# A first stage with a longer table ring, a normalisation split around the gates, and new orders on three engines

## The reference, cut to what matters

```python
x = x + 0.5 * ffn(layernorm(x))          # 8 experts of rank 16, top-2 gates
x = x + attn(layernorm(x))               # 16 heads of 16, relative positions
x = x + 0.5 * ffn(layernorm(x))

def ffn(x):                              # tokens x 256
    topw, sel = top_k(x @ Wg, 2)         # Wg 256x8
    cw = sum(one_hot(sel) * softmax(topw))
    return einsum('ter,erd->td', einsum('td,edr->ter', x, A) * cw[..., None], B)

def attn(w):
    q, k, v = w @ Wq.T, w @ Wk.T, w @ Wv.T   # split into 16 heads
    rp = sin_table(2 * L - 1, 256) @ Wr.T    # the projected table of positions
    s = (q + u_bias) @ k.T + rel_shift((q + v_bias) @ rp.T)
    return softmax(s / 4) @ v
```

## Time and profile before

| | us |
|---|---|
| median of three runs | 3110.54 |
| lowest, highest | 3108.45, 3118.55 |
| profiled execution, device time | 3110.02 |
| its span in the trace | 3108.2 |
| start of phase 1, of phase 2 (TensorE's F1) | 71.50, 98.13 |
| start of phase 8 (TensorE's P1) | 264.21 |
| last store issued by stage one | 287.70 |
| TensorE, VectorE, ScalarE, GpSimd busy, share of the span | 93%, 85%, 80%, 75% |

### The profile page before, as it was taken

One profiled execution on the slowest core, in us unless ns is written; L12 is line 12 of the kernel. 1 busy time (PEld: TensorE's weight loads), 2 busy tenths in 40 slices (PEclk: granted clock), 3 DMA queues, 4 the chain that ended last, 5 costly groups with the idle time before them and its releaser, 6 DMA issues. The chain is left out here.

```text
span 3108.2 us, 110074 instructions
## 1 busy us (share of the span) xinstructions
PE 2887.8 (93%) x40768; PEld 2036.2 (66%) x40768; DVE 2630.9 (85%) x5042; ACT 2500.7 (80%) x3854; POOL 2315.8 (75%) x4135
## 2 busy tenths in 40 slices
PE   6674699999999999999999999999999999999966
PEld 3452377777777777767677777777776767677645
DVE  4763399998999999989898999999998989899977
ACT  3443689888888898978888888889888988898832
POOL 4443888888888888878887888888887888788820
PEclk8886699999999999999999999999999999999987
DMA  6446888888888888878888888888888888888751
GB/s 202 153 130 164 203 218 229 223 231 219 225 226 228 226 228 223 229 206 223 230 221 224 224 230 228 226 221 231 228 227 213 227 229 225 218 229 227 208 155 55
DMA packets 290292, 657.40 MB, mean 212 GB/s; under 512 B 189536, under 2 KB 256992, under 8 KB 272352
## 3 DMA queue, kind: packets, MB, share of 16 engines
q0 software_dynamic: 190960, 526.89, 64.5%
q1 hardware_dynamic: 98800, 123.38, 13.7%
HBM read 77.19 MB, written 46.14 MB: 40 GB/s over the span
## 5 line engine op out<-in xcount | busy, mean ns | idle before, releaser
L834 POOL DMA_DIRECT2D score<-score x3999 | 2183.4, 549 | 499.6 <-ACT score L1093 430.2
L1091 ACT COPY score<-pos_bank 128x512 f32<-128x512 f32 x2048 | 1104.7, 597 | 280.2 <-PE pos_bank L967 278.2
L1101 ACT ACTIVATE score<-score,low 128x1024 f32<-128x1024 f32 x1024 | 1197.0, 1170 | 34.0 <-DVE low L1154 30.7
L1163 DVE COPY prob_t<-pt_bank 128x512 f32<-128x512 f32 x1792 | 1161.1, 683 | 5.1 <-PE pt_bank L1033 4.9
L1033 PEld LDWEIGHTS pt_bank<-ident_sb,score 128*128 128x128 f32 x8192 | 952.4, 142 | 217.1 <-issue 45.3
L1033 PE MATMUL pt_bank<-ident_sb,score 128*128 128x128 f32 x8192 | 1085.3, 275 | 9.0 <-issue 7.0
L1154 DVE CUSTOM_DVE_ANT_0 score<-ac_bank,score 128x1024 f32<-128x1024 f32 x512 | 626.8, 1224 | 253.6 <-PE ac_bank L1019 125.1
L1154 DVE CUSTOM_DVE_ANT_0 score<-ac_bank,score,low 128x1024 f32<-128x1024 f32 x512 | 657.0, 1283 | 57.2 <-PE ac_bank L1019 48.4
L967 PE MATMUL pos_bank<-pos,qv 96*32 96x512 bf16 (+15 forms) x12160 | 659.8, 317 | 28.7 <-DMA qv<-qv_parts 25.6
L1047 PE MATMUL acc_bank<-prob_t,vs 128*32 128x128 f32 x16384 | 664.4, 279 | 4.9 <-issue 4.8
L1019 PE MATMUL ac_bank<-ks,qu 96*128 96x512 bf16 x2048 | 623.1, 386 | 37.0 <-DVE low L1154 36.3
(11 more groups left out here) (94 smaller groups left out, 870.7 us busy)
## 6 DMA issues: line engine op xcount, KB each, us to landing
score<-score POOLq DMA_DIRECT2D x3937, 129.5 KB, 5.1
pos<-pos_parts SPq DMA_DIRECT2D x96, 128.0 KB, 8.3
qv<-qv_parts SPq DMA_DIRECT2D x192, 64.0 KB, 7.2
ks<-k_parts SPq DMA_DIRECT2D x192, 64.0 KB, 7.1
qu<-qu_parts SPq DMA_DIRECT2D x192, 64.0 KB, 7.3
v_heads<-v_sb SPq DMA_DIRECT2D x8, 1024.0 KB, 6.0
vs<-v_heads SPq DMA_DIRECT2D x32, 256.0 KB, 7.8
pos_parts<-part SPq DMA_DIRECT2D x16, 384.0 KB, 3.7
```

What stands on the lines that cost most here:

```text
L834: pool.dma_start(shifted(odd, s, groups, 0), shifted(odd, s, groups, QUAD - 1 - s))\
L1091: act.copy(score[:, at + f, c * BANK:(c + 1) * BANK], ring(m)[:, :]).then_inc(pos_out, 1)
L1101: act.activation(cols, cols, ACT.Exp, bias=low[:, slot(k), NH - 1:NH], scale=-1.0)\
L1163: dve.tensor_copy(prob_t[:, c, :], PT[c % 2][:, :]).then_inc(copied, 1)
```

## The change

The table's ring gets four chunks in place of two. Chunks 0 to 3 are loaded at the start, and the load of x's later parts no longer hangs on a table load. VectorE no longer waits for the ffn's weights before the first norm of group 0.

In a phase, TensorE's order becomes F1 F2 P1 q0 q1 F3 k0 F4 k1 V, with the wait for the lane's V copies put between F1 and F2. ScalarE's order becomes A1, the root of lane b's next first norm, exponential, N1, taken 0, part 0, taken 1, A3, parts 1 to 3, taken 2, part 4, taken 3, part 5, the root of lane a's second norm, V copies. VectorE's order becomes: statistics and variance of lane b's next first norm, the ten gate steps, reciprocal and normed tokens of that first norm (with a new wait, `free`, for lane b's P1, which reads the same buffer), rests 0 to 3, Y, statistics and variance of lane a's second norm, rests 4 and 5, its reciprocal and normed tokens.

```diff
-        def layer_norm(dve, B, S, base, no, tile, normed):
+        def layer_norm(dve, B, S, base, no, tile, normed, free=None):
 ...
             dve.wait_ge(chain, base + (2 * TG + 1))
+            if free is not None:
+                dve.wait_ge(*free)
             for t in range(TG):
 ...
-            pos_sb = s1("pos_sb", [P, 2, KT, BANK])
+            NPS = 4
+            pos_sb = s1("pos_sb", [P, NPS, KT, BANK])
 ...
                 load_pos(1)
+                load_pos(2)
                 load_x(1)
+                load_pos(3)
 ...
                 for c in range(NPC):
-                    if c + 2 < NPC:
+                    if c + NPS < NPC:
                         sp.wait_ge(pos_projected, (c + 1) * KT)
-                        load_pos(c + 2)
-                        if c % 2 == 0:
-                            load_x(2 + c // 2)
+                        load_pos(c + NPS)
+                    if c % 2 == 0 and 2 + c // 2 < len(X_PARTS):
+                        load_x(2 + c // 2)
 ...
                     if n:
                         pe.wait_ge(S["proj_out"], n * NPJ)
-                        pe.wait_ge(S["v_out"], n * TG)
 ...
-                    yield from ffn_pe(pe, LB[lane], S, n, w_in_sb, w_out_sb)
+                    steps = ffn_pe(pe, LB[lane], S, n, w_in_sb, w_out_sb)
+                    next(steps)
+                    yield
+                    if n:
+                        pe.wait_ge(S["v_out"], n * TG)
+                    yield from steps
 ...
-                    for which in (first, second, first, second, second, second, first, second, first, second, second):
+                    for which in (first, first, second, second, second, first, second, first, second, second, second):
 ...
                     B, S = LB[lane], LS[lane]
+                    if n + 1 < ROUNDS:
+                        root(act, B, S, 2 * n + 3)
+                    yield
                     for kt in range(KT):
 ...
+                    taken(0)
+                    part(0)
+                    taken(1)
+                    yield
+                    for j in (1, 2, 3):
+                        part(j)
+                    taken(2)
+                    part(4)
+                    taken(3)
+                    part(5)
+                    yield
 ...
-                    if n + 1 < ROUNDS:
-                        root(act, B, S, 2 * n + 3)
 ...
-                    for which in (first, second, first, second, first, second, first, second):
+                    for which in (first, second, first, second, second, first, second, first, second):
 ...
+                    ahead = first_norm(b[0], b[1] + 1) if b[1] + 1 < ROUNDS else iter(())
+                    after = second_norm(*a) if a is not None else iter(())
+                    next(ahead, None)
+                    next(ahead, None)
                     for _ in range(GATE_STEPS):
                         next(up, None)
-                    for _ in range(3):
+                    finish(ahead)
+                    for _ in range(4):
                         next(rest)
                     finish(up)
-                    after = second_norm(*a) if a is not None else iter(())
-                    next(rest)
                     next(after, None)
-                    next(rest)
                     next(after, None)
                     finish(rest)
                     finish(after)
-                    if b[1] + 1 < ROUNDS:
-                        finish(first_norm(b[0], b[1] + 1))
-
-                dve.wait_ge(w_loaded, 16 * 4)
 ...
                 finish(first_norm(0, 0))
+                dve.wait_ge(w_loaded, 16 * 4)
```

More of the change, by code:

```diff
@@ L308, in build_program @@
             w_proj_loaded, wr_loaded = sem("w_proj_loaded"), sem("wr_loaded")
-            pos_loaded = [sem(f"pos_loaded{i}") for i in range(2)]
+            pos_loaded = [sem(f"pos_loaded{i}") for i in range(NPS)]
             pos_projected, pos_proj_out = sem("pos_projected"), sem("pos_proj_out")
@@ L340, in load_pos @@
                 def load_pos(c):
-                    sp.dma_start(pos_sb[:, c % 2],
+                    sp.dma_start(pos_sb[:, c % NPS],
                                  pos_t[:, c * BANK:(c + 1) * BANK].rearrange("(k p) n -> p k n", p=P))\
-                        .then_inc(pos_loaded[c % 2], 16)
+                        .then_inc(pos_loaded[c % NPS], 16)
                 def load_x(i):
@@ L407, in pos_item @@
                     if m == 0:
-                        pe.wait_ge(pos_loaded[c % 2], 16 * (c // 2 + 1))
+                        pe.wait_ge(pos_loaded[c % NPS], 16 * (c // NPS + 1))
                     if i >= 4:
@@ L412, in pos_item @@
                         last = pe.matmul(PB["bank"][i % 4][:, :], lhsT=wr_sb[:, kt, m * P:(m + 1) * P],
-                                         rhs=pos_sb[:, c % 2, kt, :], start=(kt == 0), stop=(kt == KT - 1))
+                                         rhs=pos_sb[:, c % NPS, kt, :], start=(kt == 0), stop=(kt == KT - 1))
                     last.then_inc(pos_projected, 1)
@@ L509, in project, with taken, part @@
                         act.wait_ge(pos_rest1, NPI)
[L510 to L522, removed]
+                    def taken(i):
+                        act.wait_ge(S["projected"], n * NPJ + (i + 1))
+                        act.copy(B["proj"][:, i, :], B["bank"][(2, 3, 0, 1)[i]][:, :]).then_inc(S["proj_out"], 1)
+                    def part(j):
+                        i = j % KT + (KT if j >= 2 * KT else 0)
+                        act.wait_ge(S["proj_out"], n * NPJ + (i + 1))
+                        act.wait_ge(S["stored"][j], stored_by(lane, j, n))
+                        act.activation(B["part"][:, j, 0, :], B["proj"][:, i, :], ACT.Identity,
+                                       scale=1.0 if j < 2 * KT else -1.0,
+                                       bias=bias_sb[:, j // KT, i:i + 1] if j < 2 * KT else 0.0).then_inc(S["part1"], 1)
+                    taken(0)
[9 more added lines that the diff above has]
+                    yield
                     for t in range(TG):
@@ L587, in first_norm @@
                     dve.wait_ge(x_loaded[[i for i, (a, b) in enumerate(X_PARTS) if a <= g < b][0]], 16)
-                    yield from layer_norm(dve, LB[lane], LS[lane], n * NSTEP, 2 * n + 1, x_tile(lane, n), LS[lane]["normed"])
+                    yield from layer_norm(dve, LB[lane], LS[lane], n * NSTEP, 2 * n + 1, x_tile(lane, n), LS[lane]["normed"],
+                                          (LS[lane]["norm2_tp"], n * KT) if n else None)
                 def gates(lane, n):
```

## The result

The changed kernel takes 3071.67 us (median of four runs, 3062.22 to 3073.70); the kernel before, run beside it as well, 3114.55 (3108.45 to 3124.07). The ratio is 0.9863, with a 95% interval of 0.9841 to 0.9885: a gain of 43 us where 59 were forecast, and the time lies 0.7 us above the range. The profiled execution took 3073.70 us with a span of 3071.8.

What follows compares the result with a forecast made beforehand. It took a phase as a chain passing between engines, none full, and the prologue as limited by table chunks. Savings of 34.6 + 4.8 + 1.5 + 18.0 = 58.9 us gave 3051.5 us, range 3041 to 3071.

Steps and rivals of the forecast that it cites:

- part 1: Phases 2 to 6 of stage one: each falls from 28.42 to 21.5 us under the new order, saving 34.6 us.
- The first rival: TensorE's clock falls between P1 and q0, costing up to 3.1 us in phases 1 to 7: 3062 to 3073 us, chance 0.22.
- Part 2: Phase 7, which has no next first norm: it falls from 23.98 to 19.2 us, saving 4.8 us.
- part 3: Phase 8, projections only: the first rest and GpSimd's chain of six come earlier, saving 1.5 us, bounds 0 and 3.
- Part 4: Prologue and phase 1: phase 2 starts at 80.0 in place of 98.0, saving 18.0 us, from 14 to 21.
- no wait for `pos_sb`: Prologue, a sign that the forecast is right: TensorE's waits of 10.44 and 8.32 us for table chunks go.
- the Trainium skill's rule on transposes: P1: transposes do not bring the full clock; by it the sum would lose up to 3.1 us in seven phases.
- GpSimd does not let go: Rival denied here: GpSimd is done before the second norm, its tiles cost 1.4 us; 13 us less, 3039, chance 0.08.
- it is not the whole: Rival denied here: an unseen order holds the phases at about 28 us, only the prologue's 18 remain; 3092, chance 0.05.
- the last rival: Slower: VectorE stops at `free` before the first norm's tiles until P1; 9.8 us in seven phases for 3120, chance 0.02.

Runs made afterwards that it cites:

- the run with transposes: The changed kernel with 22 transposes of 128x128 added behind P1 in phases 2 to 6; 3063.3 us, ratio 0.9849.
- the ring alone: The kernel before with only the four-chunk ring, its loads and the moved weights' wait, phase orders as before; 3091.6 us, ratio 0.9940.
- the orders alone: The changed kernel with the prologue of before (ring of two chunks, loads and weights' wait where they were); 3083.2 us, ratio 0.9907.
- the run with six matmuls: The changed kernel with six matmuls of 128x512 added behind P1 in phases 2 to 6; 3072.0 us, ratio 0.9875.

## Why the prediction was wrong

By the spans, in us saved:

| term | forecast | measured |
|---|---|---|
| prologue and phase 1 (to phase 2) | 18.0 | 98.13 − 83.50 = 14.6 |
| phases 2 to 6 | 34.6 | 142.10 − 120.82 = 21.3 |
| phase 7 | 4.8 | 23.98 − 19.84 = 4.1 |
| phase 8, to stage two's first matmul | 1.5 | 40.50 − 39.49 = 1.0 |
| sum | 58.9 | 41.1 |
| stages two and three | 0 | −4.7 |

**The step that failed** is in part 1: "So the price is 0 to 3.1 us a phase, on the path", and behind it "3.6 is nearer to the row that kept its pace (1.2 off) than to the one with 5.05 (1.5 off); I take 0". The standing was sized rightly (3.6 forecast, 3.42 measured) and the price per phase lay inside its bounds (1.8 to 3.0), but the choice between the bounds was wrong, in every one of the five phases with the long standing: q0 and q1 ran at half clock there. The runs that fill it give back 24.16 − 22.34 = 1.82 a phase, 9.1 us of the 13.3 that are missing in phases 2 to 6. It is less than q0 and q1 lose, 2.5 on average: with the filling, Y stands right behind rests 1 to 3, and these take 2.96 to 3.03 us there where the changed kernel has 2.43. The first rival named this mechanism with its place, 3062 to 3073 us and a chance of 0.22. The measured time lies in it, but that is in part luck: the clock cost 9.1 us in five phases, where the rival had 11 to 22 in seven, and the other terms below make up the difference. What I argued against it, that TensorE had worked for some 20 us before, did not protect it. The nearest row by idle time of the matmuls themselves (5.05 us, 1.45 off, against 1.62, 1.98 off) was the one at half pace, and I went round it by a second measure.

**The rest of part 1** held in its mechanism. F1 and F2 are done before the other lane's tiles, `free` is never the releaser (no first-norm tile of phases 1 to 6 stands idle before it), first-norm tiles go at 1.38, second-norm tiles at 3.58 beside GpSimd. q0 came 4.57 after VectorE's last tile (132.43 to 137.00), for 4.75. With the clock kept the phase is 22.34, for 21.5: rests 4 and 5 beside GpSimd cost 2.25 where I had 1.4. That is the other 4.2 us. Y comes 0.7 late as well, behind the slower rests 1 to 3, and the variance costs 0.23 where I had 1.12; these two nearly cancel.

**Part 2 and part 3** are right within 0.7. **Part 4** was 3.4 short. Part 10 waited for its slot as the step has it, and came at 43.47 where the step has 42.0; TensorE starts phase 1 at 56.10, for 54.9, and takes 5.7 us for F1 and F2, nearly all of it at half clock, so that P1 is at 62.25 and q0 at 65.40 (1.0 us had been allowed for that). The sign "no wait for `pos_sb`" is not met: the standing of 10.44 and 8.32 us is gone, but two smaller waits for chunks are left.

```profile
39.09 3.70 PE L417 MATMUL bank_one<-pos_sb,wr_sb 128*128 128x512 f32 x8 [1.57 <-DMA pos_sb<-pos_t]
...
46.55 5.17 PE L417 MATMUL bank_one<-pos_sb,wr_sb 128*128 128x512 f32 x8 [3.76 <-DMA pos_sb<-pos_t]
```

Stage one thus falls 17.8 us short of the forecast: 13.3 in phases 2 to 6, 3.4 in part 4, 0.7 and 0.5 in parts 2 and 3.

**The transposes.** The sum went without the Trainium skill's rule on transposes, and the run with transposes shows that this was right: in all five phases either filling of the standing behind P1 kept the clock.

**Rivals.** GpSimd does not let go; the ring alone gives 19 us by the time, so it is not the whole; `free` has no wait. In the last rival F1, P1 and F2 in a line take 5.5 us (126.88 to 132.38) and not 6.2; nothing hangs on it here. What stays open is stages two and three: 2803.5 us from stage two's first matmul to the end in the profile of before, 2808.1 in that of the change, and 2799.6 to 2812.4 in those of the seven other kernels, which run the same instructions there. No trace tells what moves them, and the profiled execution's 36.3 us (3110.02 − 3073.70) differs by it from the 41.1 of stage one.

## What to carry to other kernels

When a reordering closes a long wait, look for the short one that it opens on TensorE: here the matmuls behind 3.4 us of standing ran at half pace, and moving 1.1 us of copies ahead of a small chain (root, table load, exponential) brought the end of stage one 24 us forward. Where two rows bound an unknown and the estimate lies between, the forecast should carry part of the price in the sum. And a step that waits for a store's slot holds all that stands behind it on its engine, so what the other engines need goes ahead of it.

## What the runs showed of the hardware

TensorE's clock can be lost in a loop that is busy otherwise. Ahead of phase 2 of the changed kernel it had been full for over 20 us (1.00 in every slice from 63.76 to 86.00), with no standing over 1.64 us before P1, and it still fell to half behind P1 (0.77 from 86.00 to 88.01, 0.50 from there to 93.00). In phase 4 it was 0.96 from 133.60 to 135.00 and 0.50 from there until about 141.7, so that q0 and most of q1 ran at half, for 4.7 us. Of the shorter stands between P1 and q0, 1.64 us kept q0 and q1 at 3.70 (phase 1 of the changed kernel) and so did 2.46 (phase 1 of the orders alone), but 0.94 did not always: it stood before 3.70 in the changed kernel's phase 7 and before 5.22 in that of the run with six matmuls.

The fall can lag behind the standing: with the ring alone TensorE stood for 5.02 us at a granted 1.00 and lost it only some 0.3 us after it had begun to work again. Filling the standing with transposes or with three matmuls kept q0 and q1 at 3.70 equally. A float32 matmul of 128x512 shows as two records of 0.43 us each (x12 for six, 5.15 us).
